# An attention and FFN kernel: three weight sums and the constant rows on GpSimd, and a reordered end of the attention

## The reference

```python
Q, K, V = (proj(Wq), proj(Wk), proj(Wv))
att = jnp.einsum('bhqd,bhkd->bhqk', Q, K) * (1.0 / math.sqrt(Dh)) + b[0]
att = jax.nn.softmax(att * m + (1.0 - m) * NEG_INF, axis=-1)
y = jnp.einsum('bhqk,bhkd->bhqd', att, V)
...
def weight_quant(w):
    s = 1.0 / jnp.clip(jnp.mean(jnp.abs(wf)), EPS, None)
    return (jnp.clip(jnp.round(wf * s), -1.0, 1.0) / s)
def activation_quant(x):
    s = 127 / jnp.clip(jnp.max(jnp.abs(xf), axis=-1, keepdims=True), EPS, None)
    return (jnp.clip(jnp.round(xf * s), -128, 127) / s)
...
h = jax.nn.silu(bit_linear(y, w_gate)) * bit_linear(y, w_up)      # 1024 wide
x = x + bit_linear(rms_norm(h, ln_weight), w_down)
```

## Time and profile before

| | us |
|---|---|
| median of 3 runs | 168.88 (168.17 to 168.94) |
| the profiled execution, its own time | 168.71 |
| its span, first to last instruction | 166.9 |
| TensorE busy | 147.3 |
| VectorE busy | 137.3 |
| ScalarE busy | 125.3 |
| GpSimd busy | 98.7 |

### The profile page before, as it was taken

One profiled execution on the slowest core, in us unless ns is written; L12 is line 12 of the kernel. 1 busy time (PEld: TensorE's weight loads), 2 busy tenths in 40 slices (PEclk: granted clock), 3 DMA queues, 4 the chain that ended last, 5 costly groups with the idle time before them and its releaser, 6 DMA issues.

```text
span 166.9 us, 4106 instructions
## 1 busy us (share of the span) xinstructions
PE 147.3 (88%) x1395; PEld 68.8 (41%) x1402; DVE 137.3 (82%) x199; ACT 125.3 (75%) x255; POOL 98.7 (59%) x181
## 2 busy tenths in 40 slices
PE   6969996998999999999999999988789757999883
PEld 3645553433333433433443333323123323766772
DVE  6789997497999989789898998953679666999972
ACT  3041468599899899889889888878699937598970
POOL 5889618508608618508889869523052559779930
PEclk9999999699999999999999999999999995699999
DMA  3984996636246236623322000000000000010112
GB/s 117 299 180 122 266 246 200 161 77 199 57 109 189 45 80 197 182 71 100 76 72 70 0 3 7 5 4 5 0 0 4 0 2 0 0 35 31 33 63 94
DMA packets 20124, 14.19 MB, mean 85 GB/s; under 512 B 2160, under 2 KB 19080, under 8 KB 20104
## 3 DMA queue, kind: packets, MB, share of 16 engines
q1 hardware_dynamic: 17480, 11.76, 25.2%
q10 hardware_dynamic: 2624, 2.17, 4.9%
HBM read 6.17 MB, written 1.07 MB: 43 GB/s over the span
## 4 chain that ended last, share of the span: by engine, by line
PE 61%; ACT 13%; issue 7%; DVE 7%; POOL 5%; ACTq 2%; DMA 2%; DVEq 0%; POOLq 0%
PE y_ps L1061 14%; PE s_ps L1022 13%; ACT probs L578 8%; PE t_ps L1041 6%; PE s_ps L1152 5%; PE t_ps L1171 4%; PE t_ps L998 3%; PE t_ps L1082 3%; PE y_ps L1102 2%; POOL h_m L530 2%; ACTq L286 2%; PE y_ps L1191 2%; PE t_ps L1007 2%; DMA q_st<-nm_rows 2%; PE t_ps L1191 2%
## 5 line engine op out<-in xcount | busy, mean ns | idle before, releaser
L938 DVE TENSOR_REDUCE maxes<-s_ps 128x4 f32<-128x1024 f32 x64 | 75.8, 1217 | 7.8 <-PE s_ps L1022 7.6
L578 ACT ACTIVATE probs<-t_ps 128x512 f32<-128x512 f32 x118 | 65.9, 591 | 10.0 <-PE t_ps L1041 7.8
L1041 PE MATMUL t_ps<-q_st,k_st 64*128 64x256 bf16 x236 | 43.0, 276 | 4.6 <-ACT probs L578 1.9
L1022 PE MATMUL s_ps<-k_st,q_st 64*128 64x256 bf16 x256 | 45.3, 276 | 0.1
L1061 PE MATMUL y_ps<-probs,v_pad 128*18 128x256 f32 x512 | 39.1, 388 | 0.2 <-ACT probs L578 0.2
L1022 PEld LDWEIGHTS s_ps<-k_st,q_st 64*128 64x128 bf16 x256 | 15.9, 94 | 29.0 <-issue 14.7
L1152 PE MATMUL s_ps<-w_q,ffn_x 128*128 128x512 bf16 x59 | 17.5, 396 | 7.3 <-DVE hid L872 4.4
L445 POOL TENSOR_SCALAR nm_parts<-maxes 128x16 bf16<-128x16 f32 x16 | 3.3, 209 | 29.7 <-DVE maxes L938 24.0
L1041 PEld LDWEIGHTS t_ps<-q_st,k_st 64*128 64x128 bf16 x236 | 14.0, 94 | 9.5 <-ACT probs L578 4.3
L512 POOL TENSOR_TENSOR hw<-hid,ln_bc 128x512 f32<-128x512 f32 x8 | 10.2, 1272 | 12.3 <-DVE hid L861 10.4
L1061 PEld LDWEIGHTS y_ps<-probs,v_pad 128*18 128x18 f32 x512 | 9.6, 96 | 13.9 <-issue 11.7
(11 more groups left out here) (114 smaller groups left out, 242.7 us busy)
## 6 DMA issues: line engine op xcount, KB each, us to landing
q_st<-parts SPq DMA_DIRECT2D x48, 64.0 KB
k_st<-parts SPq DMA_DIRECT2D x33, 64.0 KB
w_f<-in_wgT ACTq DMA_DIRECT2D x2, 512.0 KB, 5.4
...
```

The costliest lines, as they stand in the source:

```text
L578: act.activation(probs[:, t % NP_RING].rearrange("p e t -> p (e t)"), src, ACT.Exp, scale=SCALE)\
L938: dve.tensor_reduce(dst[:, :, s, :], s_ps[:, c % 2], AX.X, ALU.max).then_inc(s_maxed, 1)
L1022: mm = pe.matmul(s_ps[:, c % 2, i, e, :], q_st[b % RING][rows, hp, qt * P:qt * P + P], k_st[b % RING][rows, hp, :], start=True, stop=True)
L1041: mm = pe.matmul(t_bank(bank["t", t])[:, e * T:e * T + T], k_st[b % RING][rows, hp, kt * P:kt * P + P], q_st[b % RING][rows, hp, :], start ...
```

## The change

Four things change. (1) Weight sums 3, 4 and 5 leave ScalarE. GpSimd folds each in stages 1, 2 and 3 behind negate_maxes(n + 1, 0): |w| as 2 max(w, 0) - w, then halves added onto each other down to 128 columns in h_m, which is free there; VectorE sums these 128 in front of slot 1 of the next stage. The total moves from slot (3, 5) to (4, 3), and the scales from (3, 7) to (4, 5). (2) The constant rows of batch 3 and later are issued by GpSimd, in the same place of its list, ahead of the fold, and have semaphores of their own. SyncE keeps those of batches 0 to 2. (3) From slot 3 of stage 7 on, TensorE's gate(u) stands in the odd slot 2u + 1, behind the T scores. (4) Behind the stages VectorE takes hidden_steps(1) earlier, scale_y(7) later, and the late scales from GpSimd; ScalarE rounds the last y later.

```diff
-WEIGHT_SUM_SLOTS = {(-1, 5): 0, (-1, 7): 1, (0, 6): 2, (1, 6): 3, (2, 6): 4, (3, 3): 5}
-WEIGHT_TOTAL_SLOT = (3, 5)
+WEIGHT_SUM_SLOTS = {(-1, 5): 0, (-1, 7): 1, (0, 6): 2}
+FOLDED_SUMS = {1: 3, 2: 4, 3: 5}
+FOLD_END_SLOTS = {(2, 1): 3, (3, 1): 4, (4, 1): 5}
+WEIGHT_TOTAL_SLOT = (4, 3)
...
+            def fold_weights(q):
+                m, half = divmod(q, 2)
+                step = 5 * (q - 3)
+                pool.wait_ge(w_in[q], 16)
+                if q > 3:
+                    pool.wait_ge(folds_summed, q - 3)
+                w = w_f[:, m, 1024 * half:1024 * half + 1024]
+                pool.tensor_scalar(h_m[:, 0, 0:1024], w, 0.0, 2.0, ALU.max, ALU.mult).then_inc(folded, 1)
+                pool.wait_ge(folded, step + 1)
+                pool.tensor_tensor(h_m[:, 0, 0:1024], h_m[:, 0, 0:1024], w, ALU.subtract).then_inc(folded, 1)
+                pool.wait_ge(folded, step + 2)
+                pool.tensor_tensor(h_m[:, 0, 0:512], h_m[:, 0, 0:512], h_m[:, 0, 512:1024], ALU.add).then_inc(folded, 1)
...
+            def load_constant_rows(b):
+                if b < RING:
...
+                else:
+                    pool.wait_ge(unit_ready, unit["t", 16 * (b - RING + 1) - 1] + 1)
+                    pool.dma_start(q_st[b % RING][MAX_ROWS], zeros6[:, :, :].to_broadcast([6, NHP, T]))\
+                        .then_inc(later_rows_in[b % RING], 16)
+                pool.wait_ge(bias_stored, 16)
+                pool.dma_start(k_st[b % RING][BIAS_ROWS],
+                               bias_scr[b].rearrange("i k t -> (i k) t").unsqueeze(1).to_broadcast([6, NHP, T]))\
+                    .then_inc(later_rows_in[b % RING], 16)
...
                 if has(n + 1):
                     negate_maxes(n + 1, 0)
+                if n >= 0 and has(n + 3):
+                    load_constant_rows(n + 3)
+                if n in FOLDED_SUMS:
+                    fold_weights(FOLDED_SUMS[n])
...
+            def sum_folded(q):
+                dve.wait_ge(folded, 5 * (q - 2))
+                dve.tensor_reduce(w_abs[:, q:q + 1], h_m[:, 0, 0:P], AX.X, ALU.add).then_inc(folds_summed, 1)
...
+                    s = slot_number(n, k)
+                    if s > 1 and s % 2:
+                        gate(s // 2)
                     if not has(n + 1):
                         due_values(n, k)
...
-                    s = slot_number(n, k)
-                    if s >= 0 and s % 2 == 0:
-                        gate(s // 2)
+                    if s == 0:
+                        gate(0)
...
                         if u == 5:
                             weight_high_half(2)
+                            hidden_steps(1)
...
             hidden_maximum(AHEAD - 1)
-            scale_y(B - 1)
-            hidden_steps(AHEAD - 2)
             for b in range(AHEAD, B):
                 gate_times_up(2 * b)
                 hidden_steps(b - 1)
                 gate_times_up(2 * b + 1)
                 weight_high_half(b)
+                if b == AHEAD:
+                    scale_y(B - 1)
+                    scale_late_tokens()
```

More of the change, by code:

```diff
@@ L14 @@
 BIAS_ROWS = slice(5 * SLOTS + 7, 11 * SLOTS, SLOTS)
-LOADS = 2 * len(SPLITS) + 2
+LOADS = 2 * len(SPLITS)
 SCALE = 1.0 / DH ** 0.5
@@ L258, in adaln_ffn_kernel @@
         last_hm_done = sem("last_hm_done")
+        folded = sem("folded")
+        folds_summed = sem("folds_summed")
         late_scales = sem("late_scales")
+        first_rows_in = [sem(f"first_rows_in{r}") for r in range(RING - 1)]
+        later_rows_in = [sem(f"later_rows_in{r}") for r in range(RING)]
         hT_ready = sem("hT_ready")
@@ L301, in load_high @@
         def load_high(queue, b, side):
+            if b >= RING:
+                queue.wait_ge(unit_ready, unit["t", 16 * (b - RING + 1) - 1] + 1)
+            elif b:
+                queue.wait_ge(q_zeroed, b + 1)
+                queue.wait_ge(k_zeroed, b + 1)
             queue.wait_ge(hi_ready, b + 1)
@@ L370, in _ @@
             load_mask(sp, 2)
-            load_rows(2)
-            load_high(sp, 2, 0)
-            load_rows(3)
-            load_bias(3)
-            load_max_rows(0, 0)
-            load_weights(sp, 2)
-            load_bias(2)
-            load_low(sp, 2, (0, 1))
-            for n in range(B):
-                load_max_rows(n, 1)
+            for n in range(FIRST, LAST + 1):
+                if has(n):
+                    load_max_rows(n, 1)
                 if n == 0:
@@ L385, in _ @@
                     sp.dma_start(ln_bc[:, :], ln_w.partition_broadcast(P)).then_inc(ln_in, 16)
-                if n and has(n + 3):
-                    load_rows(n + 3)
+                if n == -1:
+                    load_rows(2)
+                    load_bias(2)
                 if has(n + 3):
                     load_high(sp, n + 3, 0)
+                if n >= 0 and has(n + 3):
                     load_high(sp, n + 3, 1)
@@ L394, in _ @@
                     load_weights(sp, n + 3)
-                if n and has(n + 3):
-                    load_bias(n + 3)
                 if has(n + 3):
@@ L1017, in scores @@
                         pe.wait_ge(stack_in[b % RING], 16 * LOADS * (b // RING + 1))
+                        if b < RING - 1:
+                            pe.wait_ge(first_rows_in[b], 32)
+                        else:
+                            pe.wait_ge(later_rows_in[b % RING], 32 * ((b + 1) // RING))
                     if c >= 2:
```

69 lines of the change are left out of this document (35 added, 34 removed).

## The result

| | before | after |
|---|---|---|
| median of the runs | 168.52 us (167.66 to 168.94, 4 runs) | 179.65 us (178.41 to 180.05, 4 runs) |
| ratio, 95% interval | | 1.0655 (1.0584 to 1.0725) |
| span of the profiled execution | 166.9 us | 176.6 us |
| mean granted clock of TensorE | 0.969 | 0.941 |

The changed kernel is 6.5% slower. The prediction named the side, the engine and the place, but 179.65 lies 1.15 us above its range and 4.65 above its number. Some executions of a kernel come out more than 1.5% above its fastest; all medians and ratios here leave them out.

What follows compares the result with a forecast made beforehand. The prediction took GpSimd's own period, 15.16 us against 11.56, to bound the main stages: 166.9 + 9.15 - 1.45 - 1.4 = 173.2 us of span, plus 1.8 around it, 175.0. Its range was 169.3 to 178.5 us, the forecast's own 172.5 to 177.

Steps and rivals of the forecast that it cites:

- Part 1: GpSimd's folds in stages 1 to 3: five dependent operations, 5.87 us plus gaps, 6.27 us a fold.
- The upper bound of the fold: Most a GpSimd fold could take: 6.6 us, with 1.273 doubled for 1024 columns and halved for 128.
- ScalarE's relief: Main stages, three weight sums gone from ScalarE: 3.7 us removed, 1.7 us of it felt, counted inside the 9.15.
- the folds fit: Rival in the main stages: folds and issues fit GpSimd's gaps, TensorE never waits; fully hidden 164.2 us; faster, chance 0.13.
- Part 2: Constant rows issued by GpSimd ahead of the fold: 1.53 us per pair, priced from SyncE's 0.790 and 0.742.
- SyncE's relief: SyncE's queue without the moved constant rows: loses 1.53 us of issuing per stage, costed at nothing.
- the issue is free: Rival on GpSimd's DMA issues: they cost nothing, the kernel ends at 169.2 us, no difference; chance 0.09.
- What the two do together: Folds and issues in the main stages: GpSimd's period 15.16 us against 11.56, main stages end 9.15 us later.
- The fourth wait: TensorE's wait at the second slot of stage 5, some 1.3 us, after 2.5, 3.6 and 3.6 in stages 2 to 4.
- Part 3: Last attention stage: T scores ahead of TensorE's gate remove ScalarE's idle time before its exponentials, 1.45 us off.
- Part 4: Behind the stages: hidden_steps(1) put first moves the chain up 1.85 us; VectorE's start moves some 1.4 us, the gain.
- the clock falls: Rival: TensorE's clock drops after the long waits, uncovered in stage 5, 1.7 to 3.4 us more; chance 0.12.

Runs made afterwards that it cites:

- experiment 6: Changed kernel with the fold's first instruction as (min 1e30, max 0) in place of (max 0, mult 2), factor 2 left out; 170.84 us, ratio 1.0207.
- experiment 9: Kernel before with T-score order, tail's lists and start's order, the last three weight sums on ScalarE cut to 16 columns; 163.93 us, ratio 0.9839.
- the second kernel of experiment 7: Kernel before with only the third and fourth part of the change, T-score order and tail; 163.59 us, ratio 0.9853.
- all but the folds: Changed kernel with all six weight sums on ScalarE and no fold, total and scales in their old slots; 163.65 us, ratio 0.9716.
- the kernel with the start's order and rows: Kernel before with the changed kernel's order of transfers at the start and constant and bias rows on GpSimd's queue; 166.76 us, ratio 0.9982.
- experiment 3: Kernel before with seven tensor_scalar instructions added behind GpSimd's last work, to price them alone; (max 0, mult 2) on 1024 columns took 3.63 us.
- experiment 5: Kernel before with ten more tensor_scalar pairs behind GpSimd's last work, to price them; arithmetic pairs and (min, max) took 1.04 us, the others 3.63.

## Why the prediction was wrong

- **The step that failed is the first term of Part 1's sum**: "A tensor_scalar of 2048 takes 1.89, the half is 0.95, and a tenth more for the part that doesn't halve gives 1.05". The row is a (min, max) pair and the new instruction a (max, mult) pair of the same size and type; it measured 3.65. Three times 2.6 is 7.8 us. With a pair that has the row's price, in experiment 6, the ratio falls from 1.0655 to 1.0207, some 7.5 us. The upper bound of the fold, 6.6 us, doubled columns only; no row of the trace had max beside arithmetic on GpSimd, so that term had no bound from above, and this is why the range missed. That it missed by 1.15 us only is luck: with this term alone put right the forecast would have been 182.8, and smaller misses the other way made up for 3 us. Why the pair is slow on GpSimd no run here shows.
- Part 1's other terms held: 2.36, 1.26, 0.72 and 0.45 us against 2.36, 1.27, 0.73 and 0.46. ScalarE's relief inside them was worth 0, as near as experiment 9 can tell, and not the 1.7 us that the rival "the folds fit" wanted back. The reading behind it, that the 1.68 us by which stages 1 to 4 exceed four times 11.56 are the sums' share, doesn't hold: with the sums cut short ScalarE's marks of stages 1 and 5 are 87.38 - 38.64 = 48.74 us apart, against 47.92 before.
- Part 2's pair of issues was 1.21 us against 1.53, four times 0.3 us less. The row of SyncE was near and too dear. SyncE's relief, costed at nothing, is at most small. The figure of the Trainium skill (DMA: Bandwidth & Descriptors, Latency and other measured facts), about 1 us, is one for the first byte and not for the issuing engine's time; taken for that, as the prediction did, it would have given two issues of 1 us. The trace has 0.62 to 0.65 and 0.57 us of engine time. The rival "the issue is free" fell: in stages 1 to 4 GpSimd computes nothing during an issue.
- What the two do together held in kind: TensorE waits for nm_parts at L1116 three times, 5.1, 3.9 and 4.0 us where 2.5, 3.6 and 3.6 stood, and the stage behind is 11.56 again. The fourth wait, of 1.3 us in stage 5, didn't come: there GpSimd waits for others, 0.52 us for the moved scale in front of L479 and then 0.23 for the maxima in front of the negation. Stage 4 (negate(4, 1) to negate(5, 1)) is 13.25 us by this, against 12.65 in experiment 6, where neither wait stands: 0.6 more. What of it is the scale's, which VectorE computes between the maxima, no run separates.
- Part 3 was 1.45 and is 1.48 us: y_m to tanh in that stage went from 15.92 to 14.44 us, and in the second kernel of experiment 7 the stretch from negate(7, 1) to the first h_m from 18.09 to 16.61.
- Part 4 was 1.4 and came to 3.2 in the spans. From the first h_m (127.79) to the last (157.39) it is 29.60 us before, 26.56 in the changed kernel and 26.58 in "all but the folds". One us of this is a clock that fell: before had 0.55 in 141 to 145, where the kernel with the start's order and rows has 1.00 and 28.54 us for the same stretch with the same lists. The lists themselves give 2.0, nearer to the 1.85 by which the chain moves up than to the 1.4 that I took for VectorE's start. Of the eight small operations, three are scale_y(7), which VectorE had before; only five are late scales. By the runs, parts 3 and 4 together are worth 2.5 us (1.4 to 3.5), where the forecast had 2.85.
- The 2.0 us at the start were in no sum. Before had a clock of 0.55 between 28.4 and 32.2. Three later profiles of kernels with that start's order unchanged had no such fall: negate(1, 1) stands at 36.47 in experiment 3's and at 35.72 in experiment 5's, as early as the 35.73 of the changed kernel. Two of the ten profiles with the new order had a fall. It belongs to the run more than to the order. I added my sum to one profiled execution and took its clock falls for part of the kernel.
- The rival "the clock falls" did happen, 0.50 behind each wait, and was covered in the stages as said. The last wait ended at 89.24, in stage 4 and not in stage 5; the clock is 0.50 from there to 92, and what it cost lies in the 0.6 us above. Stage 5's marks are 11.56 apart, so the 1.7 to 3.4 us didn't come.

All in all: 175.0 + 7.8 (the pair of operations) - 1.3 (issues) - 2.0 (start) - 1.8 (the rest of the tail) + 0.6 (stage 4) = 178.3, beside the 178.41 of the profiled execution.
